# Cross-attention, two layers interleaved: the second layer's weight transposes behind the first unit's scores, the last unit's affine step on VectorE

## What is computed

```python
q = jnp.einsum('bte,ef->btf', emb, Wq) + bq
k = jnp.einsum('bml,le->bme', latent, Wk) + bk
v = jnp.einsum('bml,le->bme', latent, Wv) + bv
w = jnp.einsum('bte,bme->btm', q, k) * scale
w = jax.nn.softmax(w, axis=1)
pred = jnp.einsum('btm,bme->bte', w, v)
x = pred + emb
mu = jnp.mean(x, axis=-1, keepdims=True)
var = jnp.var(x, axis=-1, keepdims=True)
return (x - mu) * jax.lax.rsqrt(var + EPS) * gamma + beta
```

## Time and profile before

| | |
|---|---|
| median of 3 runs | 1055.21 us (1053.56 to 1056.88) |
| the profiled execution | 1051.85 us |
| its span, first to last instruction | 1049.8 us |
| TensorE busy | 1005.8 us, 96% of the span |
| mean granted TensorE clock | 0.979 of full speed |

### The profile page before, as it was taken

One profiled execution on the slowest core, in us unless ns is written; L12 is line 12 of the kernel. 1 busy time (PEld: TensorE's weight loads), 2 busy tenths in 40 slices (PEclk: granted clock), 3 DMA queues, 4 the chain that ended last, 5 costly groups with the idle time before them and its releaser, 6 DMA issues.

```text
span 1049.8 us, 24861 instructions
## 1 busy us (share of the span) xinstructions
PE 1005.8 (96%) x6984; PEld 943.7 (90%) x6984; DVE 867.8 (83%) x2593; ACT 668.2 (64%) x1873; POOL 566.0 (54%) x519
## 2 busy tenths in 40 slices
PE   6687999999999999999999999999999999999984
PEld 5677999999999999999999999999999999999973
DVE  3456888889988988898888888998898888888763
ACT  1325677667666776677666766766667667666643
POOL 0013465665555656655556566555565665555654
PEclk9698999999999999999999999999999999999997
DMA  7834344444544444445444443444444444444101
GB/s 137 190 88 79 84 103 101 95 83 99 109 91 103 103 97 97 80 98 108 92 104 103 101 96 78 98 106 93 103 103 101 95 79 100 103 95 96 48 18 35
DMA packets 391215, 99.59 MB, mean 95 GB/s; under 512 B 324993, under 2 KB 375041, under 8 KB 391169
## 3 DMA queue, kind: packets, MB, share of 16 engines
q1 hardware_dynamic: 388528, 99.02, 43.9%
q10 hardware_dynamic: 2640, 0.01, 0.2%
HBM read 84.29 MB, written 14.68 MB: 94 GB/s over the span
## 4 chain that ended last, share of the span: by engine, by line
PE 90%; SPq 3%; DVE 2%; issue 2%; POOL 2%; ACT 1%; DMA 1%; ACTq 0%; DVEq 0%; POOLq 0%
PE oq_bank L595 27%; PE score_bank L571 8%; PE score_bank L572 8%; PE score_bank L576 8%; PE pv_bank L626 6%; PE pv_bank L621 5%; PE pv_bank L622 5%; PE oq_bank L547 5%; PE oq_bank L542 5%; PE oq_bank L543 5%; PE t_bank L507 3%; PE oq_bank L601 2%; PE t_bank L524 1%; SPq L332 1%; PE pv_bank L453 1%
## 5 line engine op out<-in xcount | busy, mean ns | idle before, releaser
L595 PE MATMUL oq_bank<-probs,raw 125*128 125x224 f32 x1536 | 316.2, 356 | 6.3 <-ACT probs L762 6.3
L595 PEld LDWEIGHTS oq_bank<-probs,raw 125*128 125x128 f32 x1536 | 283.8, 192 | 8.4 <-ACT probs L762 4.5
L753 ACT ACTIVATE probs<-probs,neg_max 125x224 f32<-125x224 f32 x384 | 180.6, 472 | 141.8 <-DVE neg_max L963 141.7
L1146 POOL TENSOR_TENSOR psum<-probs 125x672 f32<-125x672 f32 x64 | 103.2, 1613 | 306.7 <-ACT probs L762 306.7
L571 PE MATMUL score_bank<-qT_hi,cT_hi 128*125 128x224 f32 x768 | 198.9, 286 | 3.0 <-ACT cT_hi L710 1.6
L572 PE MATMUL score_bank<-qT_hi,cT_lo 128*125 128x224 f32 x768 | 188.4, 272 | 0.0
L762 ACT ACTIVATE probs<-probs,rsum 125x224 f32<-125x224 f32 x384 | 153.3, 471 | 13.6 <-DVE rsum L971 12.4
L1189 POOL TENSOR_TENSOR y_out<-z,gamma_row 112x512 f32<-112x512 f32 x63 | 94.4, 1519 | 117.2 <-ACT z L786 117.2
L571 PEld LDWEIGHTS score_bank<-qT_hi,cT_hi 128*125 128x125 f32 x768 | 144.7, 188 | 7.6 <-issue 3.1
L576 PE MATMUL score_bank<-qT_lo,cT_hi 128*125 128x224 f32 x768 | 146.5, 272 | 0.0
L572 PEld LDWEIGHTS score_bank<-qT_hi,cT_lo 128*125 128x125 f32 x768 | 145.0, 189 | 0.0
(11 more groups left out here) (96 smaller groups left out, 2070.7 us busy)
## 6 DMA issues: line engine op xcount, KB each, us to landing
raw<-in_ctx_dram SPq DMA_DIRECT2D x64, 375.0 KB
cb<-in_ctx_dram SPq DMA_DIRECT2D x256, 92.0 KB
xb<-in_x_dram SPq DMA_DIRECT2D x512, 28.0 KB, 1.7
x<-in_x_dram SPq DMA_DIRECT2D x32, 448.0 KB, 3.6
out_dram<-y_out SPq DMA_DIRECT2D x31, 448.0 KB, 6.6
y<-in_L_xattn_Wq_dram SPq DMA_DIRECT2D x4, 512.0 KB, 6.7
cb<-in_ctx_dram SPq DMA_DIRECT2D x128, 3.5 KB
x<-in_L_xattn_Wk_dram SPq DMA_DIRECT2D x2, 512.0 KB, 8.7
```

The costliest lines, as they stand in the source:

```text
L595: ins = nc.tensor.matmul(o, raw[0:MP, u.slot, c, cols], probs[0:MP, u.par4, c, :], start=(c == 0), stop=(c == MC - 1))
L753: ins = act.activation(probs[0:MP, u.par4, c, :], probs[0:MP, u.par4, c, :], ACT.Exp, bias=neg_max[0:MP, u.par4, c:c + 1], scale=-1.0, acc ...
L1146: pool.tensor_tensor(psum3[0:MP, :, :], probs[0:MP, u.par4, 0:HALF, :], probs[0:MP, u.par4, HALF:MC, :], ALU.add).then_inc(psum3_done, 1)
```

## The change

`transpose_weights(1)` moves on TensorE from ahead of unit 0's scores to behind them, directly ahead of `fold_beta`. `WqT_out(1)` moves on VectorE from ahead of `turn_ctx(a, 2)` to behind `score_max(a, 5)`. `WkT_out(1)` moves on ScalarE from ahead of `exps(a(-1), 0)` to behind `exps(a(-1), 1)`. At the end, `finish` runs for both halves of the last unit on VectorE, and GpSimd does neither; SP waits for VectorE's two results.

```diff
@@ store
-                    sp.wait_ge(ln_done, u.n(m=2, add=-1))
+                    sp.wait_ge(last_ln_done, 1)
                     sp.dma_start(rows[:, 0, :], ...)
-                    sp.wait_ge(last_ln_done, 1)
+                    sp.wait_ge(last_ln_done, 2)
                     sp.dma_start(rows[:, 1, :], ...)
@@ TensorE, turn
                 score_product(a(+0), 1)
                 score_product(a(+0), 2)
                 if j is None and i == 0:
+                    transpose_weights(1)
                     fold_beta()
                     fold_weights(1)
...
                 q_product(a(+1), 1)
-                if j is None and i == -1:
-                    transpose_weights(1)
                 o_product(b(+0), 0)
@@ ScalarE, turn
                 if j is None and i == 1:
-                    WkT_out(1)
                     Wv_hi_part(0)
                 exps(a(-1), 0)
...
                 exps(a(-1), 1)
                 if j is None and i == 1:
+                    WkT_out(1)
                     A_hi_part(1)
@@ finish
-                dve.wait_ge(last_zg_done, 1)
+                dve.wait_ge(last_zg_done, h + 1)
@@ VectorE, turn
                 q_lo(a(+0), 1)
-                if j is None and i == 0:
-                    WqT_out(1)
                 add_eps(a(-1))
...
                 score_max(a(+0), 5)
                 if j is None and i == 0:
+                    WqT_out(1)
                     add_beta_to_bq()
@@
             turns(dve, turn)
+            finish(Unit(LAST), 0)
             finish(Unit(LAST), 1)
@@ GpSimd, scale and add_beta
-                if u.j is None and u.u == LAST and h == 1:
+                if u.j is None and u.u == LAST:
                     return
```

## The result

| | before | changed |
|---|---|---|
| median of 12 runs | 1054.11 us | 1058.17 us (1055.97 to 1063.21) |
| ratio to before | 1 | 1.0038, 95% interval 1.0023 to 1.0053 |
| profiled execution, its span | 1051.85, 1049.8 us | 1063.21, 1061.2 us |
| TensorE busy | 1005.8 us | 1019.5 us |

The changed kernel is 0.38% slower, 4.0 us. The profiled execution of the changed kernel is the slowest of its twelve and that of before one of the fastest, so the spans lie 11.4 us apart. Whoever subtracts these two traces explains 7 us that most runs don't show. The ratios of the experiments leave out two stray executions, one of 2523 us (tail_only) and one of 5815 us (x_behind).

What follows compares the result with a forecast made beforehand. TensorE was taken as busy nearly the whole span, so only its start and end could move. 3.7 (start of L465) + 0.4 (clock) - 0.7 (end) = +3.4 us on 1055.21 gives 1058.6 us, range 1054.5 to 1062.5.

Steps and rivals of the forecast that it cites:

- The scores hide in the idle stretch, and nothing is gained by it: Prologue, TensorE: scores start at 32.8 instead of 41.78, filling the 5.47 us wait for Wq; eight transposes done by 41.
- VectorE waits for `xb`, behind its own reordered program: Prologue: VectorE reaches `turn_x` at about 39, waits until `xb` lands at 44.4; the Wq copies stand behind it.
- +3.7 us for the start of L465: Fold's one-column products on TensorE start at 50.65 instead of 46.93; bounds +2.6 and +3.9.
- +0.4 us for the clock: Fold on TensorE: late return of the high clock costs between 0 and 3.6 us; +0.4 taken.
- The rival that named it: Fold: low clock lasts through L465 into L453, L465 doubles; net about +6.6 us, 1061.8; chance 0.22.
- -0.7 us for the end: Last unit: four VectorE instructions of 0.70 us end at 46.1 instead of 46.77; bounds -0.4 and -0.9.
- The sum: Whole kernel: start of L465, clock and end together give +3.4 us, 0.32% more.
- The other rivals: Prologue: shift partly given back, net 0 to +2 us (0.15); or `xb` doesn't hold VectorE, 1051.8 to 1052.6 (0.10).
- The Trainium skill's clock rule: Prologue: idle TensorE drops to 1.2 GHz until sustained matmul work; transposes and early L465 at half pace, +3.9 to +7.5.
- The rule on the shared port: End: VectorE and GpSimd lock each other out of their shared port; removing that would win 1.3 us.
- The 0.54 us per instruction: End, VectorE: work within the add once GpSimd ended at 46.23; four at 0.54 would end at 45.5.

Runs made afterwards that it cites:

- tail_only: The kernel before with only the new end, both halves of the last unit finished on VectorE; ratio to before 0.9991 (0.9972 to 1.0010).
- x_behind: The changed kernel with VectorE's `turn_x` of unit 2 behind the Wq copies; ratio to before 1.0008 (0.9995 to 1.0021).
- x_and_wk: The changed kernel with `turn_x` of unit 2 behind the Wq copies and ScalarE's Wk copies ahead of `xT_hi`; ratio to before 0.9951.
- late_after: The changed kernel with SP issuing x of unit 2 and layer 1's three rows ahead of the sixteen `xb` transfers; ratio to before 1.0075.
- after: The first profile of the changed kernel, from the slowest of its twelve executions; 1063.21 us.
- after_again: A second profile of the changed kernel, nothing altered; 1058.3 us.
- prologue_only: The changed kernel with the old end; ratio to before 1.0040 (1.0024 to 1.0057).
- late_before: The kernel before with SP issuing x of unit 2 and layer 1's three rows ahead of the sixteen `xb` transfers; ratio to before 1.0012.
- warm: The changed kernel with the four transposes of part 1 made eleven times over, 40 more than needed; ratio to before 1.0022.

## Why the prediction was right

The median of 1058.17 us lies 0.4 from the forecast of 1058.6. The sign holds, and so does the wait that it comes from. That the number is so close is partly luck: the median of before was 1054.11 in the twelve runs, 1.1 below the one that the forecast was added to, and against it the change is 4.0 us, not 3.4. Its terms did not all hold, and their errors partly cancelled.

- *The scores hide in the idle stretch, and nothing is gained by it.* Right. The first product ran at the low clock in 2.6 us (34.17 to 36.80), the eight transposes behind them.
- *VectorE waits for `xb`, behind its own reordered program.* Right, and the best part of the forecast: landing at 44.9 (44.4 forecast), Wq copy at 46.17 (46.0), part 2 at 47.00 (46.8), L465 at 50.74 (50.65). x_behind, x_and_wk and late_after show that the landing of `xb` holds the fold. What the prediction didn't say is that it does so through ScalarE too, which alone would hold L465 to 47.8.
- *+3.7 us for the start of L465.* Too large. The end point was right, the starting point was the earliest of four profiles with the old prologue: 46.93, 47.62, 47.63, 48.03, mean 47.55. Against the mean of after, after_again and prologue_only, 50.38, it is +2.8.
- *+0.4 us for the clock.* The term that was mis-sized. L465 lasted 6.99 us in all three profiles of that prologue, and 3.64 to 5.52, mean 4.52, in the four with the old one: +2.5. The step that failed is the time of the clock's return. The prediction carried the distance from the row at 40.1 over to 50.1, just ahead of L465; in the changed kernel the high level came back at about 62.8, and only in late_after ahead of L465. The rival that named it had it at 0.22 and priced the whole at +6.6; its mechanism took place, its total did not, for part of this cost was being paid before as well.
- *-0.7 us for the end.* The measured value is -1.07. The instructions took 0.69, inside my bounds, and the later ones overlap a little, so the store left 0.77 earlier behind z. The rest is the transfer: it took 2.2 us to land instead of 2.5, with its neighbour 1.33 us ahead instead of 0.55. That the neighbour is the reason was not tried by itself.
- *The sum.* 2.8 + 2.5 - 1.1 = +4.2, beside 4.0 measured (2.4 to 5.6). The ends of the prologue lie further apart, 70.8 and 64.6 in the mean of the same three and four profiles, since products behind L465 ran at the low clock more often too; with the end that makes +5.1, still inside the interval. One of the four, late_before, has other transfers; without it the old prologue ends at 63.9 and the sum is +5.8, just outside. So few profiles fix each term to a microsecond or so, no better. The other rivals fell: nothing was given back later, since the middle doesn't depend on the prologue, and `xb` did hold VectorE.
- *The Trainium skill's clock rule* ("TensorE: Matmul & The Clock Gate", Part 1) was weighed as +3.9 to +7.5 for the first two terms; measured against the mean profile they are +5.3. The trace agrees with the rule that an idle array loses the high level: the granted clock was 1.00 at 40.5 to 43.5 us, 0.82 over the idle stretch and 0.50 behind it. The rule deserved more than +0.4. It does not tell the whole: with the old prologue the clock fell in L465 or just behind it too, with no idle stretch over 0.35 us there. *The rule on the shared port* ("SBUF — State Buffer", "Who interferes with whom") agrees in kind with the 1.15 and 1.63 us that are gone. The 0.54 us per instruction that I worked out from it was wrong: it is 0.69. With 0.69 us of work behind GpSimd's ends (1044.56 and 1046.23) VectorE's two would have ended at 1045.25 and 1046.92; they ended 0.14 and 0.15 us sooner, so not all of the work stood still.

What stays open is why the middle takes 979 to 983 us in executions of one kernel. It is a good part of the spread of the times, and no edit here touched it.

## What to carry to other kernels

When a step moves behind others in an in-order program, list every wait between its old and its new place: here the idle stretch of 5.47 us went, and one of 5.36 us for a transfer that had been hidden before took its place; moving the Wq and the Wk copies ahead of that wait turned +0.4% into -0.5%. An idle stretch of TensorE can cost more than its length: behind it L465 took 6.99 us in three profiles of three, and 3.73 where products filled it, though 4.55 in late_after. And before two traces are subtracted, check where each one's execution lies among the runs of its kernel, and profile each more than once.

## What the runs showed of the hardware

- The same 16 one-column products, 32 instructions, took 3.64 to 3.73 us at the high clock and 6.98 to 6.99 at the low one; eight 128x128 transposes 1.04 to 1.16 and 1.94.
- 48 transposes in a row, 5.40 us at the high clock, followed by an idle 1.40, did not keep the level: the next transposes began at 46.87, and it fell at about 48.4. With 26 instructions of 256 columns, 5.78 us in all, and an idle 0.54, it held through L465. Which of the two differences decides, the instructions or the idle time, was not tried.
- Idle time is not needed for a fall. Ten profiles began L465 at the high level (all but after, after_again, prologue_only and warm), and in each the clock fell within L465 or less than 0.4 us behind its end, with TensorE idle for at most 0.35 us in between. In the first profile of before that is 1.00 until 50.3 us and 0.50 from 50.4.
- A product of 256 float32 columns was two instructions of 0.219 us each at the high clock (10.53 us for the 48 of 24 products).
- An instruction with two float32 inputs of 112x512 in SBUF cost VectorE 0.69 us alone and 1.15 and 1.63 us beside GpSimd's instructions on SBUF.
